# A comparison ramp in a PSUM bank, and five banks instead of six for the feed-forward items of a graph layer

## What is computed

```python
xn = layernorm(x)
x = x + rgcn(xn, src, dst, edge_type, edge_weight) + linear_attention(xn)
x = x + mixture_of_experts(layernorm(x))
# rgcn: for each destination node, the mean over (relation, node) of weighted source rows,
#       times that relation's 256x256 matrix; plus xn @ root + bias
# linear_attention: 8 heads, feature map elu(x) + 1, keys and values summed over all nodes
# mixture_of_experts: router to 6 experts, top 2; each expert 256 -> 256 -> 256 -> 256, relu between
```

## Time and profile before

| | |
|---|---|
| runs | 3066.51, 3073.10, 3073.19 us; median 3073.1 |
| profiled execution | 3066.17 us, its span 3064.7 us |
| iterations of the last stage | from 886.8 us on; the 24th starts at 2943.5 us |
| busy over the span | PE 96%, PE weight load 84%, DVE 72%, ACT 57%, POOL 56% |
| mean granted TensorE clock | 0.984 |

### The profile page before, as it was taken

How to read it: one execution, slowest core, us unless ns; L and a number is a source line. 1 busy time by engine, 2 the same in 40 slices (tenths; PEclk the granted TensorE clock), 3 DMA queues, 4 the chain that set the end, 5 groups by cost and what they waited for, 6 DMA issues and landing times.

```text
span 3064.7 us, 47258 instructions
## 1 busy us (share of the span) xinstructions
PE 2944.0 (96%) x16707; PEld 2580.0 (84%) x16708; DVE 2191.8 (72%) x5316; ACT 1759.6 (57%) x3392; POOL 1719.4 (56%) x1700
## 2 busy tenths in 40 slices
PE   6999999969989999999999999999999999999998
PEld 5888878858779988888888898889888889888887
DVE  4479664135678888877787877778777778877775
ACT  4455555523456666655566665556656656665655
POOL 1000000042367777777777777777777777777750
PEclk9999999989999999999999999999999999999999
DMA  7667677774444434444443444444444444344430
GB/s 257 254 263 269 264 273 280 281 246 165 158 129 126 120 113 128 127 133 127 122 118 115 130 131 129 122 127 115 122 127 133 130 122 130 111 122 127 132 92 11
DMA packets 182224, 473.45 MB, mean 154 GB/s; under 512 B 46934, under 2 KB 105260, under 8 KB 159747
## 3 DMA queue, kind: packets, MB, share of 16 engines
q0 software_dynamic: 80544, 221.54, 24.8%
q1 hardware_dynamic: 99248, 247.02, 22.3%
q10 hardware_dynamic: 2196, 1.86, 0.2%
HBM read 312.80 MB, written 158.29 MB: 154 GB/s over the span
## 4 chain that ended last, share of the span: by engine, by line
POOL 39%; PE 25%; issue 13%; DVE 2%; ACT 1%; DMA 1%; DVEq 0%; SPq 0%; ACTq 0%; POOLq 0%
POOL ring L1134 39%; PE bank L1644 16%; PE acc L1701 3%; PE acc L1707 2%; PE bank L1807 1%; PE acc L1716 1%; PE acc L1644 1%; DVE row_lo L1376 1%; ACT row_hi L1191 1%; DMA xk<-xt_tab 0%; PE bank L1671 0%; DVE zv L1553 0%; PE bank L1690 0%; PE bank L1757 0%; ACT ew_hi L1275 0%
## 5 line engine op out<-in xcount | busy, mean ns | idle before, releaser
L1134 POOL DMA_INDIRECT ring<-y_tab,tab x1666 | 1702.7, 1022 | 645.2 <-issue 503.0
L1204 ACT ACTIVATE h_hi<-bank,bias_t 128x512 fp32r<-128x512 f32 (+1 forms) x600 | 407.2, 679 | 282.8 <-PE bank L1644 252.2
L1484 DVE TENSOR_TENSOR h_lo<-bank,h_hi 128x512 fp32r<-128x512 f32 (+1 forms) x600 | 381.2, 673 | 225.4 <-ACT bank L1205 222.9
L769 PE MATMUL yb<-wr_hi,xhl 128*128 128x512 f32 x1568 | 508.3, 401 | 14.9 <-ACT yst L350 12.9
L1191 ACT ACTIVATE row_hi<-ring,tab 128x256 fp32r<-128x256 f32 x1091 | 452.8, 500 | 114.9 <-issue 105.8
L1376 DVE SCALAR_TENSOR_TENSOR row_lo<-ring,tab,row_hi 128x256 fp32r<-128x256 f32 x1091 | 447.8, 477 | 73.2 <-ACT row_hi L1191 73.2
L350 ACT ACTIVATE yst<-yb 128x512 f32<-128x512 f32 x392 | 229.8, 596 | 273.5 <-PE yb L769 241.9
L1205 ACT ACTIVATE bank<-bank,bias_t 128x512 f32<-128x512 f32 (+1 forms) x600 | 386.7, 644 | 0.0
L769 PEld LDWEIGHTS yb<-wr_hi,xhl 128*128 128x128 f32 x1568 | 297.7, 190 | 89.2 <-ACT yst L350 15.2
L1644 PE MATMUL bank<-ew_hi,h_hi 128*128 128x256 f32 x1176 | 347.2, 295 | 2.2 <-DVE h_lo L1484 1.8
L1644 PE MATMUL bank<-ew_lo,h_hi 128*128 128x256 f32 x1176 | 332.1, 282 | 0.0
(11 more groups left out here) (264 smaller groups left out, 5545.0 us busy)
## 6 DMA issues: line engine op xcount, KB each, us to landing
y_tab<-yst SPq DMA_DIRECT2D x97, 1024.0 KB, 4.2
ring<-y_tab,tab POOLq DMA_INDIRECT x1666, 2.8
xt_tab<-xhl SPq DMA_DIRECT2D x25, 1024.0 KB, 4.6
xk<-xt_tab SPq DMA_DIRECT2D x25, 1024.0 KB, 4.9
xc<-xt_tab SPq DMA_DIRECT2D x25, 1024.0 KB, 5.3
x<-x_tab SPq DMA_DIRECT2D x49, 256.0 KB, 3.3
xs<-in_x SPq DMA_DIRECT2D x24, 512.0 KB, 6.0
x_tab<-xs SPq DMA_DIRECT2D x24, 512.0 KB, 5.0
```

The lines of the kernel that those rows point to most:

```text
L769: last = pe.matmul(out_ap, a, b, start=(i == 0), stop=(i == len(parts) - 1))
L1134: pool.indirect_dma_start(out=out_ap, out_offset=None, in_=y_tab[:, :], in_offset=bass.IndirectOffsetOnAxis(ap=idx_ap, axis=0)).then_inc(s ...
L1204: act.activation(dest[:, m, 0:W], b[:, 0:W], ACT.Relu, bias=bias)
L1484: gone(dve.tensor_tensor(lo_[:, m, 0:W], bank[plan[kind, (e, m)][0]][:, 0:W], hi[:, m, 0:W].bitcast(F32), ALU.subtract))
```

## The change

The ramp is copied once to a PSUM bank of its own, and `one_hot` reads it there. That bank comes from the items, which go through five banks. In the key stage the third product bank is now bank 0. The other users of `iota_w` (`weighted`, the leftovers, the gates) still read it in SBUF.

```diff
-            NBANK = 6
+            NBANK = 5
             bank = [psum(pc, f"bank{i}") for i in range(NBANK)]
+            ramp = psum(pc, "ramp")
...
-            KEY_SUM, KEY_BANK = 2, 3
+            KEY_SUM, KEY_BANKS = 2, (3, 4, 0)
...
                 dve.memset(b3_raw[:, :], 0.0).then_inc(b3_zero, 1)
+                dve.tensor_copy(ramp[:, 0:NT], iota_w[:, :])
+                dve.drain()
...
-                    dve.tensor_tensor(hot_r[:, p % BUFS, 0:size, :], iota_w[:, :].unsqueeze(1).to_broadcast([P, size, NT]),
+                    dve.tensor_tensor(hot_r[:, p % BUFS, 0:size, :], ramp[:, 0:NT].unsqueeze(1).to_broadcast([P, size, NT]),
                                       rel_w[:, n % 2, t, k:k + size].unsqueeze(2).to_broadcast([P, size, NT]), ALU.is_equal)
...
-                    dve.tensor_tensor(zv[:, v % KEY_BUFS, :, 0:P], bank[KEY_BANK + v % KEY_BUFS][:, :].rearrange("p (k n) -> p k n", k=2 * KC),
+                    dve.tensor_tensor(zv[:, v % KEY_BUFS, :, 0:P], bank[KEY_BANKS[v % KEY_BUFS]][:, :].rearrange("p (k n) -> p k n", k=2 * KC),
                                       bkv_sb[:, :].rearrange("p (k n) -> p k n", k=2 * KC), ALU.add).then_inc(key_z, 1)
...
-                    in_parts(bank[KEY_BANK + v % KEY_BUFS][:, :], lambda k: xk[:, d % 2, 0, k, nodes], lambda k: xk[:, d % 2, 1, k, nodes],
+                    in_parts(bank[KEY_BANKS[v % KEY_BUFS]][:, :], lambda k: xk[:, d % 2, 0, k, nodes], lambda k: xk[:, d % 2, 1, k, nodes],
```

## The result

| | before | after |
|---|---|---|
| median of the runs | 3069.8 us (3066.4 to 3073.2, 4 runs) | 3025.7 us (3024.6 to 3028.8, 4 runs) |
| profiled execution, its span | 3066.17, 3064.7 us | 3028.82, 3027.3 us |
| the 23 iterations | 2056.7 us | 2014.1 us |
| start of the first of them | 886.8 us | 891.6 us |

The ratio is 0.986, 95% interval 0.9847 to 0.9874: faster by 44 us.

What follows compares the result with a forecast made beforehand. POOL's gathers were taken to bound the last stage, by 3.3 us an iteration over PE. Row waits and slow clock (-61.7) plus bank waits (+20.7) gave 3025.2 us profiled, 3028 taken; forecast 3012 to 3040, 8-in-10 range 3010 to 3054.

Steps and rivals of the forecast that it cites:

- The bound: Last stage: POOL's iteration of 90.0 us exceeds PE's by 3.3 us; a 13 to 15 us lead covers the first iterations.
- Step 1: Gathers under one-hot compares are no longer held up: 2.5 us an iteration off POOL, bounds 1.6 and 5.0.
- Step 2: Five banks: query item 1 waits for DVE's `w3` read-out at each of 23 boundaries, 0.9 us each, bounds 0.72 and 1.2.
- Step 3: Key stage, copy and last iteration: nothing, at most 0.5 us once for two last-iteration items with little slack.
- Sum: Last stage: -61.7 and +20.7 give -41.0 us, profiled execution 3066.2 to 3025.2; 3028 taken from 3025 to 3032.
- Row waits and slow clock: Last stage: the 61.7 us above PE's floor, from waits for low rows and PE's lowered clock, go entirely.
- the 7 us between the runs of before: Two of three timed runs lay 7 us above the profiled execution; whether these would go or stay was left unknown.
- case D: Partial gain: over 3.2 us of gather lengthening stay, or a boundary costs over 1.2 us: 3040 to 3055, chance 0.16.
- The price of the compare: DVE's one-hot compare costs the same with one input in PSUM, by 683 and 951 ns on one line.
- A: Gathers gain little, 4.4 to 5.0 us of lengthening stay and POOL stays the bound: 3055 to 3073, chance 0.09.
- B: Bank waits drop PE to 1.2 GHz, making its iteration 90.2 us: 3084 to 3091, chance 0.06.
- C: More gain: POOL free of contention and the bank wait hidden, PE's floor: 3004 to 3012, chance 0.07.

Runs made afterwards that it cites:

- five_banks_alone: The changed kernel, but the compare reads its ramp in SBUF again, so only the five banks are left: 3057.3 us, ratio 0.9973 to the kernel before.
- twice_sbuf: The kernel before with each one-hot compare done twice from the SBUF ramp, a drain between: 3137.4 us, ratio 1.0232.
- twice_psum: The changed kernel with each compare done twice from the PSUM ramp, a drain between: 3139.4 us, ratio 1.0266 to the kernel before.
- six_banks_scalar: The kernel before, six banks and ramp in SBUF, each portion's compare written as one tensor_scalar a tile: 3055.8 us, ratio 0.9979.
- turned_banks: The changed kernel with an iteration's first five items on banks 0, 3, 1, 2, 4: 3012.3 us, ratio 0.9828 to the kernel before.

## Why the prediction was right

**The bound** (POOL by rate, with a lead). Right. five_banks_alone shows it: slowing PE by 22 waits cost nothing. In the chain of the earlier trace rows the profile puts ACT's wait of 6.79 us down to issue, and that it was the gather was my reading. It fits: the page of before has 2.8 us (median) from a gather's issue to its landing, and 1483.71 + 2.8 = 1486.51, where ACT begins at 1486.52.

**Step 1, gathers.** Expected 2.5 us an iteration off, measured (57.1 - 4.5) / 23 = 2.3, and (56.9 - 50.8) / 23 = 0.3 under low rows. DVE's compare cost the same, as expected. five_banks_alone, twice_sbuf and twice_psum together show that the ramp's place is the cause. The Trainium skill, "SBUF — State Buffer", section "Who interferes with whom", infers that a `tensor_tensor` with two SBUF inputs doesn't hold up descriptor generation. For the gathers here that doesn't hold: 82.2 against 0.5 us under the same compares.

The general rule of that section of the Trainium skill, that a DVE instruction with at most one SBUF input, outside the 2-port modes, does not contend with GpSimd, fits the 0.5 us.

**Step 2, banks.** Expected: one item of 48 waits, 23 times, 0.9 us each. Measured: that item and no other, 22 times in the window and once behind it, the iteration 87.58 - 86.74 = 0.84 us longer by the query matmuls. By the waits view the idle time is 0.58 us, and some 0.3 us more is PE's busy time (87.03 us in an iteration in place of 86.70). The item itself starts 0.97 - 0.23 = 0.74 us later, where I had worked out 0.72.

**Step 3.** The last iteration went from 121.1 to 121.6 us. That looks like the 0.5 us I allowed for its two tight items, but they didn't wait. Behind the window PE's bank waits are the same in both traces, 6.8 us in five, but for one that is new:

```profile
PE bank L1647 <- DVE y L1529: 0.6, 1, 0.6
```

It is the 23rd wait of step 2. The "nothing" of step 3 was right.

**Sum.** Row waits and slow clock -61.7, as they went entirely; bank waits +19 in place of +20.7; the window -42.6 against -41.0. The profiled execution took 3028.8 us and not 3025.2: its first iteration started 4.8 us later and its last took 0.5 us more, which the sum doesn't have, and the window was 1.6 us better. For the level I chose between 3025 and 3032 and took 3028; the median is 3025.7. What the 7 us between the runs of before were stays open: the changed kernel's own runs spread over 4 us here and 7 on the second chip.

**What was lucky.** I took the low rows' share as fixed. six_banks_scalar (+29 us) and the third chip (+19 us in the changed kernel) show that it isn't. With 29 us more in the changed kernel, (4.5 + 50.8 + 2.1 + 29) / 23 = 3.8 us an iteration would have stayed, for which the prediction estimated 3038 to 3045 us, mostly my case D.

The price of the compare was luck too. I read 683 ns with an input in PSUM and 951 ns without as points of one line, but a line goes through any two points. That the ramp's place doesn't change the length only the trace after shows, 951 ns again.

**Rivals.** A (little gain) fell with the first profile. B (the clock comes down) fell too: 22 waits of 0.58 us left the granted clock at 1.00. C (PE's floor) needed only other banks for five items: turned_banks.

## What to carry to other kernels

Where POOL runs indirect gathers back to back, look at what DVE runs beside each slow one. Here instructions with two tensor inputs in SBUF cost POOL time (2.5 us an iteration under the compares), and putting one input in PSUM removed it with DVE's compare at 951 ns as before. A round robin whose period doesn't divide the number of items has one short distance in each iteration; look for that place by comparing when each buffer is read out with when it is wanted, and move it. The price of a new wait depends on who is the bound at that point: the same 22 waits stand for 19 us above PE's floor in the changed kernel and cost nothing in five_banks_alone. What taking it back is worth depends on who is next, 12 us in the window on one chip and 1 on another.

## What was unexpected of the hardware

The lengthening of gathers isn't a sum over instructions but depends on how two periodic streams meet. The same low rows cost POOL 47 to 57 us over 23 iterations in the kernel before, the changed one, five_banks_alone and turned_banks, 69 to 70 in the last and the changed one on a third chip on which a gather takes 949 in place of 946 ns, and 62 to 96 where DVE's compares were doubled or split or a portion was moved. A gather can be held over four low-row instructions, as that of 1119.00, which starts 0.42 us behind the start of a row of five (2.46 us); in rows of six, those that start 0.52 us behind the start take 1.16 us, held only to the end of the current one. Not even the place of the start decides it. In the kernel before, 17 gathers that start 0.42 us behind the start of a row of five take 2.45 to 2.47 us, and 14 that start 0.41 to 0.43 us behind the start of a row of six take 0.94 or 0.95. Why is open.
